# Self-attention on one core: the turn of a pair's normalised rows moved into the next-but-one step, and the output weights loaded at once and converted on GpSimd

## What is computed

```
xn  = layernorm(x) * gamma                 # 32 x 56 x 256
q   = rotary(xn @ Wq)                      # 16 heads x 128
k,v = rotary(xn @ Wk), xn @ Wv             # one head
p   = softmax(causal(q @ k.T / sqrt(128)))
x   = x + (p @ v) @ Wo                     # Wo: 2048 x 256
xq  = layernorm(x) @ WxqT + bq             # the first product of cross-attention
```

## Time and profile before

| | us |
|---|---|
| median of three runs | 1468.2 |
| lowest, highest | 1467.06, 1468.42 |
| the profiled execution | 1468.98 |
| its span | 1467.2 |

### The profile page before, as it was taken

One profiled execution on the slowest core, in us unless ns is written; L12 is line 12 of the kernel. 1 busy time (PEld: TensorE's weight loads), 2 busy tenths in 40 slices (PEclk: granted clock), 3 DMA queues, 4 the chain that ended last, 5 costly groups with the idle time before them and its releaser, 6 DMA issues.

```text
span 1467.2 us, 55551 instructions
## 1 busy us (share of the span) xinstructions
PE 1370.6 (93%) x25350; PEld 1187.1 (81%) x25350; DVE 1063.4 (72%) x1858; ACT 722.0 (49%) x941; POOL 446.1 (30%) x400
## 2 busy tenths in 40 slices
PE   6689889888799999999999999999999999999983
PEld 5578778777688888888888888888888888888872
DVE  4878778777335687867768786776778677677865
ACT  3444444443255555555555555555555555555540
POOL 4223322321223233333323233332323333232300
PEclk9899999999899999999999999999999999999995
DMA  6200000000031111212111121221112122111100
GB/s 155 75 1 8 24 1 29 2 15 29 20 102 45 58 48 45 62 31 76 52 55 48 45 62 31 76 58 49 48 45 62 31 76 61 46 48 45 49 2 7
DMA packets 38827, 66.79 MB, mean 46 GB/s; under 512 B 3621, under 2 KB 36834, under 8 KB 38594
## 3 DMA queue, kind: packets, MB, share of 16 engines
q1 hardware_dynamic: 38594, 63.24, 14.9%
HBM read 61.40 MB, written 1.84 MB: 43 GB/s over the span
## 4 chain that ended last, share of the span: by engine, by line
PE 70%; DVE 2%; issue 0%; POOL 0%; POOLq 0%; DVEq 0%
PE proj_ps L1337 19%; PE proj_ps L1328 19%; PE score_ps L1355 14%; PE sum_ps L1375 12%; PE side_ps L1410 2%; PE side_ps L1392 2%; PE side_ps L1424 1%; PE side_ps L1417 1%; PE side_ps L1399 0%; DVE inv L1167 0%; DVE amax L1210 0%; DVE exps L1155 0%; DVE hidden L1242 0%; DVE hidden L1253 0%; DVE sig L1252 0%
## 5 line engine op out<-in xcount | busy, mean ns | idle before, releaser
L1107 ACT ACTIVATE exps<-score_ps 125x1792 f32<-125x1792 f32 x192 | 320.5, 1670 | 419.0 <-PE score_ps L1355 419.0
L1155 DVE TENSOR_SCALAR exps<-exps,top 125x896 f32<-125x896 f32 x384 | 288.0, 792 | 18.0 <-ACT exps L1107 17.5
L1355 PE MATMUL score_ps<-spread,keys 32*125 32x112 f32 x6144 | 219.4, 279 | 0.0
L1375 PEld LDWEIGHTS sum_ps<-exps,vals 125*32 125x32 f32 x12288 | 163.8, 110 | 50.6 <-issue 34.2
L1146 DVE COPY vals<-proj_ps 125x512 f32<-125x512 f32 x192 | 128.3, 688 | 104.6 <-PE proj_ps L1337 104.1
L1355 PEld LDWEIGHTS score_ps<-spread,keys 32*125 32x125 f32 x6144 | 185.2, 183 | 15.4 <-issue 0.4
L1375 PE MATMUL sum_ps<-exps,vals 125*32 125x56 f32 x12288 | 192.5, 215 | 2.6 <-DVE exps L1155 2.5
L1050 POOL TENSOR_TENSOR low<-raw_early,high 128x500 fp32r<-128x500 f32 x64 | 100.9, 1585 | 231.1 <-issue 115.4
L1050 POOL TENSOR_TENSOR low_early<-raw_early,high_early 128x500 fp32r<-128x500 f32 x62 | 104.3, 1690 | 172.1 <-issue 104.0
L1099 ACT ACTIVATE keys<-proj_ps,b_k 128x500 f32<-128x500 f32 x192 | 130.2, 678 | 52.1 <-PE proj_ps L1328 52.1
L300 POOL TENSOR_TENSOR swapped<-swapped,sin 128x448 f32<-128x448 f32 (+1 forms) x72 | 88.6, 1233 | 162.0 <-ACT swapped L547 161.9
(11 more groups left out here) (163 smaller groups left out, 2690.3 us busy)
## 6 DMA issues: line engine op xcount, KB each, us to landing
raw_early<-in_ctxT SPq DMA_DIRECT2D x64, 500.0 KB, 3.9
raw<-in_ctxT SPq DMA_DIRECT2D x32, 500.0 KB, 3.5
w_q<-in_attn_Wq SPq DMA_DIRECT2D x4, 512.0 KB, 9.2
raw_early<-in_attn_Wo SPq DMA_DIRECT2D x2, 1024.0 KB, 12.8
out<-y_out SPq DMA_DIRECT2D x16, 112.0 KB, 2.0
rows<-in_x SPq DMA_DIRECT2D x1, 1344.0 KB, 18.5
raw_early<-in_ffn_gate_wT SPq DMA_DIRECT2D x1, 1024.0 KB, 4.9
raw_early<-in_ffn_val_wT SPq DMA_DIRECT2D x1, 1024.0 KB, 4.9
```

The costliest lines, as they stand in the source:

```text
L1107: nc.scalar.activation(exps[t % 2][:, :, :, :].rearrange("p h r n -> p r h n"), score_ps[0:TILE, :, 0:2 * QW].rearrange("p r (h n) -> p r ...
L1155: nc.vector.tensor_scalar(tile, tile, LIMIT_LO, top[:, n, at:at + 1], ALU.max, ALU.min)\
L1355: ins = nc.tensor.matmul(score_ps[0:TILE, r, to:to + HE * S], keys[c % 2][32 * r:32 * r + 32, k, (at + half) * TILE:(at + half + 1) * TILE ...
L1375: ins = nc.tensor.matmul(sum_ps[32 * h:32 * h + VW, g, :], vals[c % 2][:, at + half, HJ * g + h, :], exps[t % 2][:, half, r, col:col + S], ...
```

## The change

In the loop over pairs norm2_turn(p - 1) at the end of step p becomes norm2_turn(p - 2) right behind scores(p); ScalarE's copy out of PSUM goes to the same place of its own order, and the list of units, which hands out the banks, is changed alike. VectorE's and GpSimd's parts of the normalisation (norm2_rows, power) stay where they are. In steps 14 and 15 cross_q(p - 2) moves behind turn(p, 0), and in step 15 the turn of pair 14 stands before out_heads(15, 1).

The second half of the output weights is loaded into a part of queries, which is not in use yet, right behind the first. Both halves are converted by a tensor_copy on GpSimd: the first behind the last product with sin before the loop, the second behind the first such product of step 0. ScalarE's conversions are gone. VectorE's two subtractions move behind normalise(0) and to the end of step 0.

```diff
@@ units
+            if p >= 2:
+                units += [("norm2", p - 2)]
             units += more[0:1]
-            if p >= 2:
+            if p >= 2 and more:
                 units += [("xq", p - 2)]
...
+            if not more:
+                units += [("xq", p - 2)]
             units += more[2:4]
-            if p:
-                units += [("norm2", p - 1)]
...
-        units += [("xq", PAIRS - 2), ("y", PAIRS - 1), ("norm2", PAIRS - 1), ("xq", PAIRS - 1)]
+        units += [("norm2", PAIRS - 2), ("xq", PAIRS - 2), ("y", PAIRS - 1), ("norm2", PAIRS - 1), ("xq", PAIRS - 1)]
+        def w_o_raw(n):
+            return w_raw[:, :] if n == 0 else queries[:, :, :].rearrange("p c n -> p (c n)")[:, 0:half_o * D]
@@ sync
             out_weights(0)
+            out_weights(1)
             sp.dma_start(w_xq[:, :, :], dram["xattn_WqT"].rearrange("(c p) n -> p c n", p=P)).then_inc(small2_in, 16)
             sp.dma_start(b_xq[:, :], dram["xattn_bq"]).then_inc(small2_in, 16)
-            sp.wait_ge(w_o_split, 1)
-            out_weights(1)
@@ gpsimd
+            def out_weights(n):
+
+                pool.wait_ge(wo_in[n], 16)
+                nc.gpsimd.tensor_copy(w_oh[:, half_o * n:half_o * (n + 1), :].rearrange("p h n -> p (h n)"), w_o_raw(n))\
+                  .then_inc(w_o_high, 1)
...
             sines(("kv", 1))
+            out_weights(0)
...
-                for name in more[0:2]:
+                for name in more[0:1]:
+                    sines(name)
+                if p == 0:
+                    out_weights(1)
+                for name in more[1:2]:
                     sines(name)
@@ vector
             rotary(("kv", 1))
-            out_weights(0)
...
                 normalise(p)
+                if p == 0:
+                    out_weights(0)
                 for name in more[1:2]:
                     rotary(name)
-                if p == 0:
-                    out_weights(1)
...
                 for b in range(2):
                     out_low(p, 1, b)
+                if p == 0:
+                    out_weights(1)
@@ scalar
             swap(("kv", 1))
-            out_weights(0)
...
+                if p >= 2:
+                    normed2_out(p - 2)
                 for name in more[0:1]:
                     swap(name)
-                if p >= 2:
+                if p >= 2 and more:
                     queries_out(p - 2)
                 exps(p)
-                if p == 0:
-                    out_weights(1)
...
                 probs_out(p, 0)
+                if not more:
+                    queries_out(p - 2)
...
                 probs_out(p, 1)
+                if p == PAIRS - 1:
+                    normed2_out(PAIRS - 2)
...
-                if p:
-                    normed2_out(p - 1)
@@ tensor
                 scores(p)
+                if p >= 2:
+                    norm2_turn(p - 2)
                 for u in more[0:1]:
                     heads_q(g + 1, u)
-                if p >= 2:
+                if p >= 2 and more:
                     cross_q(p - 2)
...
+                if not more:
+                    cross_q(p - 2)
                 out_heads(p, 0)
...
+                if p == PAIRS - 1:
+                    norm2_turn(PAIRS - 2)
                 out_heads(p, 1)
-                if p:
-                    norm2_turn(p - 1)
```

More of the change, by code:

```diff
@@ L254, in out_weights @@
             def out_weights(n):
-                sp.dma_start(w_raw[:, :].rearrange("p (h n) -> p h n", h=half_o),
+                sp.dma_start(w_o_raw(n).rearrange("p (h n) -> p h n", h=half_o),
                              dram["attn_Wo"].rearrange("(h p) n -> p h n", p=P)[:, half_o * n:half_o * (n + 1), :])\
@@ L426, in out_weights @@
                 dve.wait_ge(w_o_high, n + 1)
-                nc.vector.tensor_tensor(w_ol[:, half_o * n:half_o * (n + 1), :].rearrange("p h n -> p (h n)"), w_raw[:, :],
+                nc.vector.tensor_tensor(w_ol[:, half_o * n:half_o * (n + 1), :].rearrange("p h n -> p (h n)"), w_o_raw(n),
                                         w_oh[:, half_o * n:half_o * (n + 1), :].rearrange("p h n -> p (h n)").bitcast(F32),
@@ L569, in out_half @@
                                out_ps[:, b, 0:AU * S].rearrange("p (h s) -> p h s", s=S)).then_inc(outT_high, 1)
[L571 to L575, removed]
             def normed2_out(p):
```

## The result

The changed kernel takes 1456.8 us (median of four runs, 1456.7 to 1457.2) beside 1468.3 for the kernel before: a ratio of 0.9924, with an interval of 0.9907 to 0.9941. It is faster by 11.5 us, where 21.7 were forecast; the fastest of all executions of the kernel before, in this comparison and in the later ones, took 1461.2 us. The forecast was 1446.5 and the time lies at the upper edge of its range.

What follows compares the result with a forecast made beforehand. TensorE and VectorE were taken to bound the kernel by waiting on each other in the loop before the block border. 13.5 + 4.5 + 4.4 - 0.5 = 21.9 us off the median 1468.2 gave 1446.3, stated as 1446.5; range 1440 to 1457.

Steps and rivals of the forecast that it cites:

- What bounds it: Loop before the block border: neither TensorE nor VectorE is full; the two in-order engines take turns at waiting.
- the turn's move frees TensorE by 2.1 us: End of each loop step: TensorE's 1.80 us stand and the 0.3 us turn leave, so kv and scores start 2.1 us sooner.
- The waits named as going: VectorE in the loop: waits for kv values (9.5 us) and scores (4.8 us) go, plus 0.35 us a step at the first q unit.
- what was named as staying: VectorE in loop steps: waits of 1.61 us for the third q unit and 0.59 us for GpSimd behind it remain.
- TensorE's stand in front of y: Loop steps: TensorE, now early, waits for a bank before y, 1.4 us at most, at no cost; slack 0.4 us.
- VectorE's queue is unchanged, so I take its waits away one by one: Loop: VectorE, late next, keeps its work and loses only waits; its step with a kv unit becomes 21.7 us.
- the terms 13.5 and 4.5 of the sum: Loop gains: 13.5 us from waits for values and scores, 4.5 us from 0.35 us at the first q unit over 13 steps.
- The 14.3 us of waits: VectorE in the loop: 9.5 us for values plus 4.8 us for scores; the upper end of the term taken as 13.5.
- Part 2, 4.4 us: Step 0, output weights: with conversions on GpSimd (2.5 us a copy) and subtractions moved, step 1 begins 4.4 us sooner.
- Part 3, -0.5 us: Last steps: moving xq and the turns loses 0.5 us, with -2 and 0 as ends.
- Clock dips, some: Rival, front of y: the clock falls in 3 or 4 steps at 2.7 us each, giving 1455 us; chance 0.22.
- Slow copies: Rival, step 0: GpSimd copies take 6.0 us each, so step 0 gains 2 us for 4.4, giving 1449 us; chance 0.08.

Runs made afterwards that it cites:

- sin1_late: The changed kernel, but in steps 1 to 13 GpSimd's product for the second q unit waits until VectorE has normalised the probabilities: 1453.1 us.
- short_after: The changed kernel with each GpSimd product with sin cut to its first 56 columns, all waits kept: 1424.2 us, one run.
- p2_alone: The changed kernel with only the new handling of the output weights; loop and last steps as in the kernel before: 1465.0 us.
- p1_alone: The changed kernel with the turn moved but the output weights handled as in the kernel before: 1457.6 us.
- act_both: The changed kernel with both conversions of the output weights on ScalarE before the loop, none on GpSimd: 1455.2 us.
- best_tail: Changed kernel with sin01_late's delays, act_both's conversions, the first subtraction behind step 0's fourth rotation, and pair 14's turn back behind the second attention product: 1446.3 us.
- sin01_late: sin1_late, with GpSimd's first-q-unit product in steps 1, 2, 4, 6, 8, 10, 12 also waiting until VectorE has subtracted the maxima: 1450.8 us.

## Why the prediction fell short

*What bounds it, and that the turn's move frees TensorE by 2.1 us:* right. The waits named as going (values, scores, 0.5 us for the first product) went, and what was named as staying (1.61 us and 0.59 us at the third q unit) stayed; TensorE's stand in front of y came, longer than I had put it, and cost nothing (sin1_late).

*"VectorE's queue is unchanged, so I take its waits away one by one":* this step failed, and with it the terms 13.5 and 4.5 of the sum: the loop gained 8.5 us for their 18.0. The instructions were unchanged, their durations were not. I had the earlier trace rows before me with a subtraction of 2.29 us and of 3.22 "with GpSimd active beside it", and read that as an item of step 0 instead of as a price on each VectorE operation whose neighbour moves. Even steps were to take 20.4 us and take 21.45, which is longer than the 21.0 before: 0.56 us of waits are gone, 0.76 us on line 418 and 0.35 on line 427 have come. Odd steps were to take 21.7 and take 21.92. Over 13 steps 9.2 us. sin1_late takes 0.53 us a step of it away by moving nothing but a product of GpSimd, and short_after takes away all: the cause is shown. The Trainium skill has the rule, in GPSIMD Engine Reference, section 1 (Specifications): GpSimd shares its SBUF interfaces with VectorE, with contention for instructions in a 2-port mode or with two inputs in SBUF. The trace agrees: lines 418 and 427 have two such inputs and stretch, line 458 goes from 0.41 to 1.23 us, and line 394, with one input in PSUM, keeps its 0.61 us beside a copy. Whether line 458, with one tensor in SBUF and two scalars, is of the first of these kinds, no run here shows. I had weighed that page for the speed of the copy alone.

A second fault lies in the same term. The 14.3 us of waits that it starts from hold 6.1 us by which they had grown in the four steps at the lower clock (waits for values of 2.79 and 2.19 us for 1.12, for scores of 1.73 and 1.58 for 0.21, and of 0.42 for none); the term leaves out 0.8 of them. To move the turn takes these away only if the clock stays up, and of that the prediction says nothing: two such steps fewer came in the profiled execution and gave 3.6 us. Without the clock the waits and the 4.5 us come to 12.7, and the steps themselves gained 4.9.

*Part 2, 4.4 us:* 0.9 came (1.2 in p2_alone), hardly more than the start varies (62.44 us in p1_alone, the same as the kernel before up to there, for 62.89). The copy was sized about right (2.5 us for 2.3 and 2.8, of which 1.9 are its own), and its neighbours at nothing. Line 411 of step 0 starts at 39.77 us, not at 38.0, as line 401 is stretched by 1.2 us and line 404 ahead of it by 0.5; lines 404, 418 and 427 follow with 0.9, 0.2 and 0.7 more than their own length, and the subtraction, put at 2.3 us, takes 3.22. Those are 4.4 us together, of which the first 0.5 had been there by 0.4 before; step 1 starts 3.5 us later than forecast. act_both gives back 1.1 us of it in step 0 and some 1.0 in front of it.

*Part 3, -0.5 us:* the stretch from step 15 to the border gained 1.8. The sign is due to the clock: the products of the last y ran at the lower level before (0.41 us in the earlier trace rows) and at full speed after (0.28), 5.6 us from the first to the last for 7.4. In p2_alone, with the last steps as before and a clock of 0.99, that stretch takes 26.1 us, 2.2 less than the changed kernel's at 0.94. Of these, 1.3 lie between the turn of the probabilities and y (7.5 us for 8.8) and are what the moves cost, for the 0.5 that I had put; best_tail shows 1.1 of it. The other 0.9 lie behind y, where the eight products of xq take 2.02 us for 1.12 at the lower clock.

*The rivals.* "Clock dips, some" named a time near the measured one, but for a mechanism that is not there: the clock fell less often than before (0.99 for 0.98 in the loop, two steps for four), and not in front of y as a habit. "Slow copies" was wrong, too: the copies were fast. The missing mechanism was none of the rivals.

*Open:* why the clock falls in some steps and not in others that look alike. It varies between executions of the same loop (292.3 and 296.8 us), so some 3.6 us of the loop's gain and the sign of the last row may not come back in another execution. The seven profiled executions with part 1 and whole products had one to three such steps, the two without it four and eight. That speaks for part 1 as what brings the higher clock, but no run shows how. It did not fall in the loop of either kernel with the products cut short, one execution each, and why not was not looked into. Why line 458 takes 0.82 us longer beside a product of which 1.07 us are left, and not 0.93 like the others, stays open too.

## What to carry to other kernels

When a wait is removed, do not only ask what is late next; lay the queues of the engines beside each other at their new times and ask which operations now run at once. A VectorE operation with two operands in SBUF that starts while GpSimd works takes longer by nearly all that GpSimd has left, 0.2 to 1.2 us here, and one that starts first doesn't. So a wait that keeps the two apart can be free or even pay, if slack stands behind it (0.53 us a step in sin1_late) and hardly pays where none does (0.17 in sin01_late). Work moved to an idle GpSimd is not free if VectorE is the bound: ScalarE, which had a hole of 3 us at that place, did it for 1.1 us less in step 0. And a wait that was read in a step at a lower clock is not a wait that a change of order removes; count such steps apart.

## What the runs showed of the hardware

- A VectorE operation with two operands in SBUF that starts inside a GpSimd product or copy takes longer by what is left of it less 0.14 us: one of 0.39 us took 1.55 us with 1.30 us of a copy left, one of 0.62 took 1.55 with 1.08 left. One of 0.41 (one operand in SBUF, two scalars) took 1.23 with 1.07 us of a product left. The cosine product, with an operand in PSUM, and the reduction kept 0.61 and 1.07 us.
- The same holds with the engines exchanged: a product takes 1.13 to 1.15 us where VectorE is the one that is stretched, and took 1.60 and 1.71 before where it started with 0.60 and 0.71 us of line 403 left.
- A copy of 2048 columns with conversion takes 1.88 us on GpSimd (short_after) and 1.90 on ScalarE; GpSimd's took 2.29 and 2.76 where they started behind a VectorE operation of two operands.
- The granted clock averaged mostly 0.92 or 0.93 over single steps, in one (p1_alone) to eight (p2_alone) steps of a loop in the nine kernels with whole products, and most of these steps took 1.0 to 1.6 us longer. In the two with the products cut no step fell below 0.98. Nothing in TensorE's work was found that would explain which.
